# A transformer block on one core: V's bias folded through the output weights into the output's bias row

## What is computed

```python
q = h @ q_w + q_b
kv = context @ kv_w + kv_b
k, v = jnp.split(kv, 2, axis=-1)
# mha: softmax(q k^T / 4) v, head by head
h = mha(q, k, v) @ cross_o_w + cross_o_b
x = x + h            # layer 1: x + h * gate_msa
```

## Time and profile before

| | us |
|---|---|
| median of 3 runs (lowest, highest) | 517.02 (516.67, 517.41) |
| the profiled execution | 519.42 |
| its span, first to last instruction | 517.4 |

### The profile page before, as it was taken

One profiled execution on the slowest core, in us unless ns is written; L12 is line 12 of the kernel. 1 busy time (PEld: TensorE's weight loads), 2 busy tenths in 40 slices (PEclk: granted clock), 3 DMA queues, 4 the chain that ended last, 5 costly groups with the idle time before them and its releaser, 6 DMA issues.

```text
span 517.4 us, 11609 instructions
## 1 busy us (share of the span) xinstructions
PE 444.6 (86%) x4274; PEld 306.6 (59%) x4274; DVE 292.1 (56%) x778; ACT 249.6 (48%) x555; POOL 184.3 (36%) x247
## 2 busy tenths in 40 slices
PE   4675958989899989889787887999999998999996
PEld 1343534645475556566565654676666665689995
DVE  6746716593948464615657767656754574434321
ACT  1441534655574546545534422566666665562221
POOL 2434322442646344615315214244343422252200
PEclk9977788999999989989989777899999999999999
DMA  7474995195725187952817203437347232200000
GB/s 226 104 104 86 171 182 142 59 123 134 160 72 97 33 131 116 113 108 61 114 38 107 58 3 98 142 80 107 76 77 107 56 76 62 73 3 18 20 18 18
DMA packets 46853, 46.17 MB, mean 89 GB/s; under 512 B 10662, under 2 KB 44966, under 8 KB 46798
## 3 DMA queue, kind: packets, MB, share of 16 engines
q1 hardware_dynamic: 44934, 45.15, 45.1%
q10 hardware_dynamic: 1864, 0.29, 0.4%
HBM read 14.63 MB, written 0.93 MB: 30 GB/s over the span
## 4 chain that ended last, share of the span: by engine, by line
PE 60%; DVE 16%; issue 9%; DMA 5%; ACT 4%; POOL 3%; SPq 3%; ACTq 0%; POOLq 0%; DVEq 0%
PE bank L462 7%; DVE nmax L951 7%; PE bank L598 7%; PE bank L578 7%; PE bank L454 6%; PE bank L561 6%; PE bank L649 5%; PE bank L488 5%; PE bank L638 5%; DMA k_stack<-fill_space 3%; SPq L1188 3%; PE bank L623 3%; DMA q_stack_all<-nm_t 2%; PE bank L508 2%; DVE xn L845 2%
## 5 line engine op out<-in xcount | busy, mean ns | idle before, releaser
L951 DVE TENSOR_REDUCE nmax<-bank 112x1 f32<-112x375 f32 (+1 forms) x288 | 142.1, 548 | 82.6 <-PE bank L561 81.4
L789 ACT ACTIVATE prob<-bank 128x448 f32<-128x448 f32 (+2 forms) x224 | 113.2, 545 | 61.6 <-PE bank L578 58.4
L561 PE MATMUL bank<-k_stack,q_stack_all 96*128 96x375 bf16 x256 | 69.1, 345 | 19.1 <-DVE nmax L951 7.0
L1090 POOL TENSOR_TENSOR fill_space<-fill_space 128x375 f32<-128x375 f32 x32 | 30.2, 946 | 100.9 <-ACT fill_space L722 100.9
L578 PE MATMUL bank<-q_stack_all,k_stack 99*128 99x112 bf16 x768 | 57.1, 220 | 7.0 <-DMA q_stack_all<-nm_t 7.0
L598 PE MATMUL bank<-prob,v_tokens 128*17 128x112 f32 (+1 forms) x1536 | 57.6, 267 | 0.1
L578 PEld LDWEIGHTS bank<-q_stack_all,k_stack 99*128 99x128 bf16 x768 | 42.7, 101 | 24.5 <-issue 13.7
L1104 POOL TENSOR_TENSOR v_tokens<-v_tokens,bias_rows_v 128x256 f32<-128x256 f32 (+1 forms) x48 | 32.8, 697 | 67.1 <-ACT v_tokens L734 67.1
L561 PEld LDWEIGHTS bank<-k_stack,q_stack_all 96*128 96x128 bf16 x256 | 24.2, 102 | 53.7 <-DVE nmax L951 28.3
L454 PE MATMUL bank<-fill_space,wkv 128*128 128x375 f32 x128 | 50.5, 521 | 2.3 <-ACT fill_space L743 2.3
L462 PE MATMUL bank<-wkv,fill_space 128*128 128x256 f32 (+1 forms) x192 | 49.4, 394 | 2.4 <-DVE v_all L922 1.6
(11 more groups left out here) (123 smaller groups left out, 666.7 us busy)
## 6 DMA issues: line engine op xcount, KB each, us to landing
...
```

Source lines behind the costliest of these rows:

```text
L561: last = pe.matmul(to[:, o:o + w], q_all[0:DEEP, q + h * N2:q + h * N2 + P], keys, start=True, stop=True)
L789: act.activation(prob[n % 4][0:rows, :], bank[SCORE_T[n % 2]][0:rows, 0:GH * T], ACT.Exp).then_inc(exp_done, 1)
L951: dve.tensor_reduce(nmax[:, g * hs:(g + 1) * hs], bank[SCORE[n % 3]][0:T, 0:hs * w].rearrange("t (h k) -> t h k", k=w), AX_X, ALU.max, neg ...
L1090: pool.tensor_tensor(kr[:, m, :], kf[:, m, :], kp[i % 2][:, 0, m, :], ALU.subtract).then_inc(krest_done, 1)
```

## The change

Nothing is added to V any more. POOL's 48 additions go, and so does the semaphore v_done; PE waits for ACT's copy of V instead. In layer 1 DVE's addition from PSUM becomes a copy. Two new steps are placed once for each layer l:

- "F", l: PE transposes the row of V's bias (two matmuls against the identity, 112 x 112 out of each 128-channel half), and ACT copies the result to a new tile vbias_t. All 112 columns are the same vector.
- "G", l: PE multiplies it by the layer's output weights (the same shape as L623), and DVE adds the product to the output's bias row, in place.

pool_base then waits for "G" in place of the bias row's transfer. F and G of layer 0 stand at (0, 3) and (0, 9), of layer 1 at (7, 8) and (7, 11), all in bank TB; of layer 2 at (12, 3) and (13, 2), in bank CX.

```diff
...
-    (7, 6): [("N", 8)], (7, 7): [("L", 8), ("n", 9)], (7, 8): [("N", 9)], (7, 9): [("L", 9)],
+    (7, 6): [("N", 8)], (7, 7): [("L", 8), ("n", 9)], (7, 8): [("F", 1), ("N", 9)], (7, 9): [("L", 9)],
...
+    (0, 3): [("F", 0)],
+    (0, 9): [("G", 0)],
+    (7, 11): [("G", 1)],
+    (12, 3): [("F", 2)],
...
+    vbias_t = sb("vbias_t", [P, CH, T])
...
+    VROW = [brow_v[0:T, 0, :], brow[2], brow_v[0:T, 1, :]]
...
+        elif kind == "F":
+            l = step[1]
+            if l == 0:
+                pe.wait_ge(rows0_in, 16)
+            elif l == 1:
+                pe.wait_ge(late1_in, 16 * LATE1)
+            else:
+                pe.wait_ge(late_in, 16 * LATE)
+            for c in range(CH):
+                last = pe.transpose(cx[:, c * T:(c + 1) * T], VROW[l][:, c * P:(c + 1) * P], ident[0:T, 0:T])
+            last.then_inc(filled[bk], 1)
+        elif kind == "G":
+            l = step[1]
+            if l == 0:
+                pe.wait_ge(wo0_in, 16)
+            else:
+                pe.wait_ge(late2_in, 16 * LATE2)
+            read_by(pe, ("F", l))
+            for c in range(CH):
+                last = pe.matmul(cx[0:T, 0:C], vbias_t[:, c, :], WO[l][:, c, :], start=c == 0, stop=c == CH - 1)
             last.then_inc(filled[bk], 1)
...
-                pe.wait_ge(v_done, NT * (i + 1))
+                read_by(pe, ("V", i, 1))
...
+        elif kind == "F":
+            l = step[1]
+            act.wait_ge(filled[bk], before + 1)
+            if l > 0:
+                fbk, fbefore = USES["G", l - 1][0:2]
+                act.wait_ge(filled[fbk], fbefore + 1)
+            act.activation(vbias_t[:, :, :], cx[:, 0:CH * T].rearrange("p (c n) -> p c n", c=CH), ACT.Copy).then_inc(read[bk], 1)
...
+        elif kind == "G":
+            l = step[1]
+            dve.wait_ge(filled[bk], before + 1)
+            if l == 0:
+                dve.wait_ge(bp0_in, 16)
+            else:
+                dve.wait_ge(late_in, 16 * LATE)
+            dve.tensor_tensor(brow[BO_ROW[l]], cx[0:T, 0:C], brow[BO_ROW[l]], ALU.add).then_inc(read[bk], 1)
...
-            dve.tensor_tensor(v_all[:, b:b + 2, :, 0:D], cx[0:T, :].rearrange("t (j h d) -> t j h d", j=2, d=D),
-                              brow[2].rearrange("t (o h d) -> t o h d", o=1, d=D).broadcast_to([T, 2, H, D]),
-                              ALU.add).then_inc(read[bk], 1)
+            dve.tensor_copy(v_all[:, b:b + 2, :, 0:D], cx[0:T, :].rearrange("t (j h d) -> t j h d", j=2, d=D)).then_inc(read[bk], 1)
...
-        elif kind == "V":
-            _, i, part_no = step
...
-            for t in ((0, 1) if part_no == 0 else (2,)):
-                v = v_sb[i % 2][0:KEYS[t], t, :, 0:D]
-                pool.tensor_tensor(v, v, brow_v[0:KEYS[t], i // B, :].rearrange("p (h d) -> p h d", d=D), ALU.add).then_inc(v_done, 1)
...
-            if a == 0:
-                pool.wait_ge(bp0_in, 16)
-            if a == 2 * B:
-                pool.wait_ge(late_in, 16 * LATE)
+            read_by(pool, ("G", a // B))
...
-            if b == 0:
-                pool.wait_ge(late_in, 16 * LATE)
+            read_by(pool, ("G", 1))
```

11 lines of the change are left out of this document (3 added, 8 removed), and 2 rows, old and new, of the table JOBS.

## The result

The kernel after took **511.82 us** (median of 20 executions, 505.84 to 515.59), the kernel before 517.64 us beside it (median of 20, 513.03 to 520.84). The ratio is 0.987, 95% interval 0.984 to 0.990; the two medians alone give 0.989, or 5.8 us. Measured again with other kernels, after stood at 0.988 (0.985 to 0.991). The ratios here leave out as slow every run over 1.5% above the fastest of its kernel, 6 of after's 20 and 11 of the 35 of before beside e1 to e4, so after's comes out lower than that of its medians and e1's and e2's higher (0.996 against 0.993, 1.000 against 0.997). My forecast was 516.4 us, a gain of 0.65, with a range down to 514.2.

A forecast was written before the change was run, and what follows sets the result against it. PE was taken as the bound in most rounds, idle only where a DVE, POOL or transfer chain is late. Terms -1.4 - 0.8 + 1.4 + 0.15 = -0.65 us gave 516.4 us, range 514.2 to 518.9.

The forecast's parts named there:

- The front, -1.4: Before round 0: without POOL's additions ahead of "h", DVE's five maxima begin 1.4 us earlier; bounds 0 to 1.5.
- I let the landing move with it in full: Before round 1: the maxima's transfer, awaited 6.98 us by PE, lands earlier by the front's whole advance.
- the front's advance is swallowed: Rival, chance 0.10: the landing at 78.85 stays, set by the transfer engines, not the trigger; 517.8 us.
- F and G of layer 0, 0: At (0, 3) and (0, 9): both stand ahead of PE's waits and cost 0; without that cover 1.4 us.
- The end of round 6, -0.8: Without POOL's additions there, PE's wait of 1.13 us before L479 shrinks by 0.8 us; bounds 0.5 and 1.13.
- The other 14 samples, 0: Their additions lie where POOL's next work waits anyway or DVE has slack; removing them gains 0.
- The copy, 0: Layer 1, L922: the copy out of PSUM takes the addition's 0.692 us; range 0 to -0.5, taken 0.
- Layer 1, +1.4: F at (7, 8), G at (7, 11): dense stretch of PE, nothing hides them, 1.4 us; bounds 0.7 to 1.5.
- Layer 2, +0.15 and a wait of 1.7: F at (12, 3) delays a chain by 0.15 us; G at (13, 2) costs 0, cutting a 2.73 us wait to about 1.7.
- PE's clock stays up: Rival, chance 0.25: with less wait before L479, a later low-clock stretch goes, saving 1.3 us more; 515.1 us.
- 0.12 "up or down": Remaining chance: several clock stretches up or down, split 0.06, 0.03, 0.03 over faster, same and slower.
- layer 0's 1.4: At (0, 3) and (0, 9): cost of layer 0's F and G if no wait covers them.

The follow-up runs named there:

- e1: The kernel before without POOL's 48 additions and without F and G; 514.18 us, 0.996 of before.
- e4: The kernel after with the context loads of place (0, 8) held until round 1's maxima have landed; 514.05 us, 0.994 of before.
- e2: The kernel after with all additions put back and G's sum thrown away, so only F and G are added to before; 515.99 us, 1.000 of before.
- e7: The kernel after once more, unchanged, for a second trace; 512.66 us, 0.988 of before.
- e13: The kernel before with F of layer 0 alone, its copy going to a tile that nothing reads; 516.64 us, 0.996 of before.
- e9: The kernel after without F and G of layer 0; 512.47 us, 0.989 of before.
- e3: The kernel before with the context loads of place (0, 8) held until round 1's maxima have landed; 517.21 us, 0.999 of before.
- e6: The kernel after with the context loads of place (0, 8) moved to (1, 0), behind sample 2's key transfers; 514.27 us, 0.993 of before.
- e12: The kernel after with POOL's three additions of sample 0 (the front) put back; 514.31 us, 0.993 of before.
- e8: The kernel before without the three additions of sample 0 (the front), the other 45 kept; 514.12 us, 0.991 of before.
- e11: The kernel after without F and G of layer 2; 509.31 us, 0.984 of before.

## Why the prediction was wrong, step by step

**The front, -1.4: right.** 1.5 us over 20 traces. The five maxima begin at 43.52 and not near 42.7 because this execution was a us late by then (the three maxima begin at 41.85, before's at 40.87); from the three maxima to the five, it is 1.67 us, forecast 1.83.

**"I let the landing move with it in full": the step that failed.** I had read that the transfer of round 1's maxima is late because of the loads, and that the loads' trigger moves with the front. Then I took the distance from trigger to landing as fixed. It isn't. From round 0's start to round 1's start the two traces of before have 27.5 and 26.9 us, the five of after 20.2, 26.2, 20.1, 23.5 and 20.1. The wait of 6.98 us, from which I let G take 1.05, was in three of five traces moved behind 5.8 us of PE's work, and is 4.9 to 5.4 us there; in e7 it is 6.04, near the 5.9 that I forecast. This term was sized 0 and measured **3.7 us** on average over rounds 0 and 1 of the five traces, 2.8 over the eight with the same program there. My rival "the front's advance is swallowed" had the same view with the sign turned round; none let the landing come earlier by more than its trigger.

What part of it has which cause is only partly settled. Shown: the transfer is issued 1.4 us earlier after round 0's start, where a low stretch of PE's clock is gone; F alone removes it (e13). Shown too: in three traces all of its packets pass ahead of sample 2's keys, and the last of them starts 3.6 to 4.0 us after the issue instead of 7.9 to 10.5. Not shown: why in these three and not in the seven others with the same distance between the two issues. e13 has the early issue and not the gain; e9 has neither F nor G in layer 0 and after's time. The order of packets between ACT's queue and SP's isn't in the program, and taking the loads away (e3 to e6) replaced the race by another wait. The Trainium skill, "DMA: Bandwidth & Descriptors", section "Queues, rings and completion order", has each transfer engine take turns between the queues that have work for it, a packet at a time. From that I would expect a small transfer on a queue of its own to pass a long one quickly. The traces show it in three of 16 cases only: 3.0 to 7.3 us to the first packet with the loads under way, 1.4 without them.

**F and G of layer 0, 0: right as to cost, wrong as to effect.** e9 is no faster than after. That filling a wait of 0.26 us could remove a stretch of low clock in round 0 did not occur to me; I had considered that for round 6 alone. Nor had I asked what G pushes back besides PE.

**The end of round 6, -0.8: 0.56.** The wait went from 1.13 to 0.57 in after, and e12, which has the other samples' additions out, shows 0.57 too. I named DVE's second L845 as next; it was ACT's L779, which I had not looked for. **The other 14 samples, 0: right.** e1 against e8 shows no gain for 45 additions. (The two rows on the chain that ended last are four additions, not two.) The rule on the shared port pair (the Trainium skill, "SBUF — State Buffer", section "SBUF: two separate sides") is borne out once more on durations: "m" (L939, now L978) fell from a median of 618 ns to 386, L845 from 654 to 410. On the time it counts in the front, where "m" took 0.85 us beside an addition and takes 0.38 now; elsewhere no gain shows (e1 against e8).

**The copy, 0: right,** 692 ns before and after. **Layer 1, +1.4: 0.8.** From the rows' distances I had 0.34 + 1.05; in place the two cost 0.8 up to the start of round 8, as in the windows above. Why less was not looked into. **Layer 2, +0.15 and a wait of 1.7:** the wait was 1.87, and F's matmuls took 0.3 us ahead of a chain that mostly covers them. Right within what rows can tell, but e11 leaves up to 3 us open, and I can't tell its place from chance.

**The rival "PE's clock stays up", 515.1 us:** its price, 1.3 us a stretch, was right, and in round 0 a low stretch did disappear with a filled wait. The place that I named was wrong. After round 6 the low stretch comes and goes between executions (before's two traces have it, and one of five of after).

Together the small terms behind round 1 come to -0.56 + 0.8 + 0.2 = +0.4 us, close to the forecast's +0.75; with the front that is a gain of 1.1. The rest of the measured 5.8 is rounds 0 and 1, and the number of low-clock stretches, which I had given 0.12 "up or down". The front's term came out at its size because it was read from rows; that the sum had the sign is partly luck, since it left out the largest term.

**The range.** Added straight, the bounds of the terms give -2.8, and +1.3 or, with layer 0's 1.4, +2.7; the "-2.6 to +1.5" of the prediction follows from neither. None of them reaches the 5.2 us between 517.02 and 511.82, because rounds 0 and 1 had no term of their own, and because the spread of executions entered only through those 0.12.

No kernel here beats after with the same result; e11 is faster in the median but leaves out layer 2's bias.
